# Shifts of the first layer norm taken two chunks ahead, between the low parts, and one GpSimd mask selection moved behind that norm

## What is computed

```
xn = (x - mean(x)) / sqrt(var(x) + 1e-5)          # row by row, over 256 numbers
s  = attention(xn)  (layer 0: q, k, v with norms, sigmoid scores, Wo, layerscale; layer 1: a bank of 2048 keys)
g  = silu(ffn(xn))  (layer 0: 16 routed experts, 4 per row, and a shared expert; layer 1: ternary MLP)
x  = x + s * g
```

## Time and profile before

| what | value |
|---|---|
| time, median of 3 runs | 1284.95 us (1284.31 to 1285.41) |
| profiled execution, its own time | 1290.11 us |
| span of its instructions | 1288.3 us, 26740 instructions |
| TensorE busy | 1226.3 us (95% of the span) |
| VectorE busy | 892.1 us (69%) |
| ScalarE busy | 555.7 us (43%) |
| GpSimd busy | 441.4 us (34%) |
| mean granted TensorE clock | 0.982 of full speed |

### The profile page before, as it was taken

How to read it: one execution, slowest core, us unless ns; L and a number is a source line. 1 busy time by engine, 2 the same in 40 slices (tenths; PEclk the granted TensorE clock), 3 DMA queues, 4 the chain that set the end, 5 groups by cost and what they waited for, 6 DMA issues and landing times.

```text
span 1288.3 us, 26740 instructions
## 1 busy us (share of the span) xinstructions
PE 1226.3 (95%) x8985; PEld 873.9 (68%) x8986; DVE 892.1 (69%) x1891; ACT 555.7 (43%) x1043; POOL 441.4 (34%) x407
## 2 busy tenths in 40 slices
PE   4889999999899999999999997999989999999998
PEld 4546667767688888866666665777756666666665
DVE  7798867565467666668889886999745455545554
ACT  5533643333266666656433333666632222222221
POOL 3232777776408450045777762331000000000000
PEclk8899999999999999999999998999989999999999
DMA  8798323333288666521455558442020111101100
GB/s 283 228 385 332 106 99 107 119 125 117 87 269 253 177 190 193 172 90 54 144 155 161 175 170 271 125 137 82 34 83 13 37 50 50 47 2 49 49 18 17
DMA packets 134047, 169.23 MB, mean 131 GB/s; under 512 B 12181, under 2 KB 121898, under 8 KB 131658
## 3 DMA queue, kind: packets, MB, share of 16 engines
q1 hardware_dynamic: 117370, 130.21, 31.0%
q0 software_dynamic: 12368, 33.70, 8.2%
q10 hardware_dynamic: 4224, 4.19, 1.0%
HBM read 84.18 MB, written 83.89 MB: 130 GB/s over the span
## 4 chain that ended last, share of the span: by engine, by line
PE 76%; issue 8%; POOL 8%; DVE 5%; ACT 2%; DMA 1%; DVEq 0%; SPq 0%; POOLq 0%; ACTq 0%
PE bank L1179 26%; PE sums L1226 24%; PE bank L1105 7%; PE sums L1115 4%; PE sums L1193 3%; POOL reg_e L820 3%; PE bank L1085 2%; POOL reg_e L835 2%; PE bank L1022 2%; PE sums L1351 2%; PE sums L1038 1%; POOL xg_d L797 1%; PE sums L1028 1%; PE sums L1057 1%; PE bank L1148 1%
## 5 line engine op out<-in xcount | busy, mean ns | idle before, releaser
L2056 DVE TENSOR_SCALAR reg_w<-reg_w 128x512 f16<-128x512 f32 x320 | 149.8, 468 | 224.5 <-ACT reg_w L1569 223.0
L1226 PE MATMUL sums<-reg_v,reg_w 128*128 128x256 f16 x2304 | 285.2, 274 | 4.1 <-DVE reg_w L1743 4.1
L1226 PEld LDWEIGHTS sums<-reg_v,reg_w 128*128 128x128 f16 x2304 | 226.7, 98 | 72.0 <-DVE reg_w L1743 4.5
L1743 DVE SCALAR_TENSOR_TENSOR reg_w<-reg_w 128x512 f16<-128x512 f32 x320 | 223.1, 697 | 11.0
L1179 PE MATMUL bank<-reg_qk,kbT 128*128 128x512 f16 (+1 forms) x768 | 188.0, 381 | 0.0
L1179 PE MATMUL bank<-reg_qk 128*128 128x512 f16 (+1 forms) x768 | 186.7, 379 | 0.0
L1569 ACT ACTIVATE reg_w<-bank 128x512 f32<-128x512 f32 x128 | 76.5, 597 | 252.2 <-PE bank L1179 245.9
L1569 ACT ACTIVATE reg_w<-bank,nlogs 128x512 f32<-128x512 f32 x128 | 88.0, 688 | 178.2 <-PE bank L1179 174.5
L815 POOL DMA_INDIRECT xg_d<-xr,icol x108 | 115.1, 1066 | 48.4 <-issue 26.4
L1179 PEld LDWEIGHTS bank<-reg_qk,kbT 128*128 128x128 f16 x768 | 75.5, 98 | 64.0 <-issue 1.1
L1179 PEld LDWEIGHTS bank<-reg_qk 128*128 128x128 f16 x768 | 74.6, 98 | 62.7
(11 more groups left out here) (239 smaller groups left out, 1805.1 us busy)
## 6 DMA issues: line engine op xcount, KB each, us to landing
xg_d<-kbT SPq DMA_DIRECT2D x18, 1024.0 KB, 5.3
xin<-xg_d SPq DMA_DIRECT2D x72, 256.0 KB, 2.8
yg_d<-xr SPq DMA_DIRECT2D x72, 256.0 KB, 2.2
reg_qk<-in_L_attn_x_dram SPq DMA_DIRECT2D x8, 512.0 KB, 8.6
sh_d<-xin SPq DMA_DIRECT2D x16, 256.0 KB, 3.1
xr<-xn_d SPq DMA_DIRECT2D x32, 128.0 KB, 2.2
reg_e<-sh_d SPq DMA_DIRECT2D x32, 128.0 KB, 2.6
moe_d<-reg_e SPq DMA_DIRECT2D x32, 128.0 KB
```

What stands on the lines that cost most here:

```text
L1226: mm = pe.matmul(a_bank[2 * i + q // 2][:, (q % 2) * D:(q % 2 + 1) * D], part[:, j % 4, q * P:(q + 1) * P], m.second(y, j), start=(j == 0 ...
L1743: ins = dve.scalar_tensor_tensor(out=out_ap, in0=in_ap, scalar=scale, in1=hi_ap, op0=ALU.mult, op1=ALU.subtract)
L2056: dve.tensor_scalar(ah[:, j % 4, :], att[:, j % 2, :], m.split, None, ALU.mult).then_inc(m.hi_done, 1)
```

## The change

Three things move, and no work is added or taken away. The shift of chunk c + 2 is now taken in iteration c, between the two low parts of chunk c; before, the shift of chunk c + 1 stood at the head of iteration c. At the start, the shift of chunk 0 stands between the bn_stats and the bn_aggr of chunk 1. And GpSimd's affine_select on the mask moves from ahead of the norm's powers to behind them, where it waits for the last low part of the norm.

```diff
@@ gpsimd @@
             pool.wait_ge(ready_id, 5)
             pool.memset(zeros, 0.0).then_inc(zero_src, 1)
-
-            pool.wait_ge(cross_made, 3)
-            pool.affine_select(out=cross_h, in_=cross_h, compare_op=ALU.is_ge, fill=0.0, base=-1,
-                               pattern=[[-P, 4], [E, TT], [0, E]], channel_multiplier=-1).then_inc(cross_made, 1)
             open_(pool, shx["lo"], ln["rs"], q4["m2"], q4["rs"], q4["rn"], pj["rs"])
...
             by(pool, NCH, 2, ln_rows)
+
+
+            pool.wait_ge(cross_made, 3)
+            pool.wait_ge(ln["lo"], at(2 * NCH - 1))
+            pool.affine_select(out=cross_h, in_=cross_h, compare_op=ALU.is_ge, fill=0.0, base=-1,
+                               pattern=[[-P, 4], [E, TT], [0, E]], channel_multiplier=-1).then_inc(cross_made, 1)
@@ vector @@
-            def moments(src, n, i, c, q, eps):
+            def moments(src, n, i, c, q, eps, between=None):
 
                 for m in range(n):
                     dve.bn_stats(stat[:, i, m, :], src(m))
+                if between:
+                    between()
                 dve.drain()
...
-            def x_moments(c):
+            def x_moments(c, between=None):
                 dve.wait_ge(x_ld[c], 16)
-                moments(lambda m: x_all[:, c, m, :], G4, c % 2, c, ln, EPS)
+                moments(lambda m: x_all[:, c, m, :], G4, c % 2, c, ln, EPS, between)
...
             x_moments(0)
-            x_moments(1)
-            shifts(0, 0, ln, 2)
+            x_moments(1, lambda: shifts(0, 0, ln, 2))
+            shifts(1, 1, ln, 2)
             for c in range(NCH):
                 i = c % 2
-                if c < NCH - 1:
-                    shifts(c + 1, 1 - i, ln, 2)
                 if c < NCH - 2:
                     x_moments(c + 2)
                 for b in range(2):
                     low_of(c, i, b, s_bank[2 * i:2 * i + 2], xT, X_S, ln["hi"], ln["lo"])
+                    if b == 0 and c < NCH - 2:
+                        shifts(c + 2, i, ln, 2)
```

## The result

The changed kernel takes 1283.09 us (median of 20 runs, 1280.11 to 1286.65), the kernel before 1285.26 us beside it (20 runs, 1283.34 to 1289.4). The ratio is 0.9985, with a 95% interval of 0.9979 to 0.9992: 2.2 us off, 1.0 to 2.7 by the interval. The forecast was 2.6 off.

The account below looks back on a forecast made before the run. VectorE bounds 60 to 97 us, then the scatters; the norm stage is a ring of waits. 1.40 + 0.12 + 0.18 + 1.23 = 2.93, less 0.3, gives 2.6 off 1284.95: 1282.3 us, range 1280.7 to 1285.1.

Parts of the forecast that it names:

- The start: First norm chunks: first shift 2.0 us earlier, part lost to chunk 2's load; bn_stats of chunk 3 come 1.40 us earlier.
- The loop: Norm's steady loop: waiting for GpSimd's power replaces waiting for ScalarE; almost no gain, 0.12 us over iterations 1 to 4.
- The end of the norm: Last shift gains 1.23 us; with the earlier gains the norm stage ends 2.93 us earlier.
- The selection: Behind the norm: the moved selection stretches one VectorE bias instruction until it ends; cost 0.3 us, bounds 0 and 1.2.
- rival (a): Behind the norm: the selection also holds the first bias instruction, from PSUM; cost 1.2 us, time 1283.2; chance 0.13.
- Rival (b): From 48.4 us on: DMAs are the bound, the first scatter stays at 133.56, time 1285.0; chance 0.10.
- rival (c): Shared expert's products: they start before TensorE's clock rises and run at 1.2 GHz, costing up to 5.3 us; chance 0.07.
- the prediction's second step: Behind 133.56 us: GpSimd's scatters hold the routed rows' load, which moves from 344.05 to 341.4 us with the first scatter.
- rival (d): The 128 scatters: their pace shifts, 1% being over 1 us; chance 0.13 on the fast side (1281), 0.05 slow (1284).

Follow-up runs that it names:

- e1: The kernel before with only GpSimd's selection moved behind the norm's powers; 1325.54 us, ratio 1.0 to the kernel before.
- e2: The changed kernel with the selection put back ahead of the norm, so only the shifts move; 1321.65 us, ratio 0.9974 to the kernel before.
- e4: The changed kernel with the shift of chunk c + 2 behind both low parts instead of between them; 1319.7 us, ratio 0.9974 to the kernel before.
- e3: The changed kernel with the selection waiting for the last bias part instead of the norm's last low part; 1319.93 us, ratio 0.9975 to the kernel before.
- e6: The changed kernel with the edits of e4 and e3, e5's products, and x chunk 2 loaded ahead of the router's weights; 1320.1 us, ratio 0.9984.
- n3: All edits of e6 with the edit of n1; 1285.41 us, ratio 0.999 to the kernel before.
- c1: The changed kernel again, no edit; 1321.19 us, ratio 0.998 to the kernel before.
- n2: The changed kernel with the same edit as n1; 1287.23 us, ratio 1.0011 to the kernel before.
- n1: The kernel before with the first attention's score scaling written as SCALAR_TENSOR_TENSOR instead of TENSOR_SCALAR; 1289.75 us, ratio 1.0029 to the kernel before.
- c2: The kernel before again, no edit; 1321.67 us, ratio 0.9998.
- e5: The changed kernel with 14 added, unused products of 128x512 in TensorE's idle times of the norm stage; 1318.75 us, ratio 0.9982.
- n4: The edits of e6 without the added products; 1332.28 us (12 runs), ratio 0.9938 to the kernel before.

## Why the prediction was right, and where it was not

**The start: right.** `ve` 0.17, the first norm at 9.13 (forecast 9.15), shift 1 at 11.12 (10.99), bn_stats of chunk 2 behind the landing at 11.58 (11.6), those of chunk 3 at 16.24 (16.27). e1 and e2 split the first shift's 2.0 us in 0.93 for the selection and 1.02 for the new place. Alone they end the norm 0.92 and 2.28 us earlier, together 2.97, not 3.2: in e2 the bn_stats of chunk 2 start at 12.21 without waiting, and with the selection moved as well they can only come forward to the landing, at 11.58. That the landing was where the earlier trace rows put it was luck: it took 6.4 to 7.7 us in the eleven profiles that issue this load at 5.02 us, and in e4 the bn_stats of chunk 2 came 1.1 us later by it.

**The loop: right.** One wait for the other, 0.62 for 0.65 us, and 4.55 us a chunk (`ve` at 18.12 and 22.67), as forecast. e4 shows that this second wait could be hidden too, and that a store's buffer is the next limit.

**The end of the norm: right.** 2.97 us for 2.93.

**The selection: right in mechanism, 0.2 for 0.3.** L1775 was held to its end and L1772 not. By the Trainium skill (SBUF — State Buffer, Who interferes with whom) a one-input VectorE instruction contends only in a two-port mode; L1772, from PSUM, agrees with 0.85 us beside the selection and 0.85 without it, and rival (a) falls with it. e3 and e2 (0.55 us with the selection elsewhere) show that it is the selection that stretches L1775. Rival (b) fell too: the first scatter moved with L1982 in all runs, 81.5 to 81.8 us behind it in twelve profiles. In e6 and n3 it was 82.5 and 82.2, with a longer wait for its rows' load, so a version that gains more begins to meet a DMA there.

**The clock, rival (c): it was real, and priced too high.** It got 0.07, at up to 5.3 us. It came in c1, e2, e3 and n2, and in n1 with the old shifts, and cost 0.9 us (c1) to 1.7 us (n1), since only part of the products fell in the low stretch. The prediction's sum for a rise at 51 us, the whole 5.3 us, was wrong: in 5.5 us at half the clock TensorE does half of what it does in 5.5 us at full clock, and loses 2.7. Nor did it come as the prediction had it, by a first rise that is late: in all five the clock had been full already and fell again, at 41 us in c1, between 44.5 and 46 in e2, e3 and n2, between 48.5 and 49 in n1. My argument against it was that TensorE's earlier work moves too. It doesn't move as a block: the profile after has waits of 2.04 and 1.95 us ahead of two products in a row of `route`, where before had 0.71 and none, and the clock rose at 39.5 us, where in before and c2 it rose at 44.

**What arrives: the step that failed.** It is the prediction's second step, that the scatters "hold the load of the routed experts' rows", with that load at 341.4 after the change. It went at 336.45. The step took the train for a fixed length and the load for what the end waits for, and both hold only in part. The table shows three cases. In one, the train is late (207.2 us or 209.9) and TensorE waits for it for 2.4 to 4.8 us: before, c2, e2, e3, e4, n1 to n3. In the second the train is short and TensorE is the bound: after, c1, e5. In the third TensorE stalls for several us on the way (train 199.5 to 202.0): e1, e6, n4.

TensorE's own way is fixed. Take its idle time off the start of the transposes, and from L1982 to there it is 291.9 to 292.3 us in ten of the eleven profiles without stalls, old shifts (before 292.14, c2 292.15) and moved ones (after 291.89, c1 292.11, e5 292.13) alike; the eleventh is n3, with 292.7 and the longer wait at its first scatter. So what L1982 gains arrives at TensorE's end of this stretch whole, and n1 and n2 show it for the first case too, up to the end of the span and in the medians. What does not stay fixed is the train, by how many scatters begin just behind a low part. That is rival (d), which I had as 1%, something over 1 us; it is 4.2 us between the profiles of before and after, and up to 10 us between others. That no profile with the old shifts has a short train and no stall, so that the second case could be compared as well, is a gap.

What the train does to the times is not shown either. Each kernel that was profiled twice had the same train twice (207.25 and 207.24, 203.08 and 203.50), which speaks for a property of the kernel; but then the changed kernel should gain more than the 2.75 us of L1982, and it measured 2.2. The executions that were not profiled, with their spread of 6 us, don't tell which trains they had.

Whether the measured 2.2 is the forecast 2.6 with noise, or 2.75 less the low clock in part of the executions, the interval of 1.0 to 2.7 doesn't tell. The mechanism up to the first scatter was right; that the number was near as well is in part luck, since the prediction had no account of the 4 us by which the train differs.

**Open.** Why a kernel's scatters meet the low parts more or less often is not settled: the kernels differ only in the first 50 us, and the count goes from 4 to 23. The stalls of TensorE in e1, e6 and n4 came in the three longest profiles (spans of 1326.8 us and more), and their cause wasn't tried.

## What to carry to other kernels

When an instruction waits for another engine, put the work that doesn't need the answer between the question and the wait, and then look which engine is asked next: here it went from ScalarE to GpSimd to a store's buffer. Move an operation that locks another engine out only to a place where the locked one has slack behind it, and name the one instruction that will be stretched. And before a profiled difference is read as the gain, compare it with the times of more executions: here 4.9 of the 7.75 us belonged to one slow execution of the kernel before. A second profile alone wouldn't have shown it, since the late train came again in c2.

## What the runs showed of the hardware

- Two kernels with the same instructions up to 170 us, and equal to 0.02 us up to 48.43 us, had TensorE at 2.4 GHz in one profile and at 1.2 in the other from about 49 us on (c2 and n1). It cost 1.70 us at L1982. The changed kernel, unedited, had it at 2.4 GHz at 46 to 47.5 us in one profile and at 1.2 in another (after and c1).
- A scatter of GpSimd that began 0.04 to 0.2 us behind a SCALAR_TENSOR_TENSOR of 128x512 with both inputs in SBUF mostly took 1.34 to 1.5 us instead of 0.96 (166 of 240 in the fourteen profiles); in 71 of the others the SCALAR_TENSOR_TENSOR took some 0.77 us instead of 0.69. Beside one with an input in a PSUM bank none of 103 took more than 0.98.
- A SCALAR_TENSOR_TENSOR of 128x512 from SBUF in place of the TENSOR_SCALAR takes 0.691 us instead of 0.453 to 0.465. The scatters' mean (1.058 us in n1, 1.066 in before, 1.074 in c2) and their train (207.24 and 207.25) hardly change.
- The train of 128 scatters took between 199.45 and 209.87 us, with nothing changed in the scatters.
- From the routed transposes to its end the kernel before took 941.4 us in one profile and 972.5 in another (before and c2), with the first and the last scatter alike to 0.02 us.
